# A decoder layer on one core: the first cross-attention stream in another order, the output scaling placed earlier, selection in halves and a final normalisation in pieces

## The reference

```python
x = _layernorm(x + self_attention(x))
# cross attention, 16 heads of 32, causal
q, k, v = (heads(x @ Wq.T + bq), heads(ctx @ Wk.T + bk), heads(ctx @ Wv.T + bv))
Srel = _skew(einsum('bhsd,ld->bhsl', q, Er))
attn = softmax(where(causal, (q @ k.T + Srel) / sqrt(32), -inf))
x = _layernorm(x + (attn @ v))
# routed feed-forward
probs = softmax(einsum('bsd,de->bse', x, Wg) + bg, axis=-2)   # over the 1024 rows
vals, idx = top_k(transpose(probs), 128)
tok = x[bidx, idx]
h = relu(tok @ w1 + b1); h = relu(h @ w2 + b2); h = h @ w3 + b3
out = _layernorm(x + zeros.at[bidx, idx].add(h * vals[..., None]))
```

## Time and profile before

| | us |
|---|---|
| median of 3 runs | 4421.03 |
| lowest, highest | 4416.5, 4429.57 |
| the profiled execution, own time | 4421.36 |
| its span, first to last instruction | 4419.6 |
| busy in it: PE, DVE, ACT, POOL | 3878.7, 2499.9, 1573.0, 908.0 |

### The profile page before, as it was taken

One profiled execution on the slowest core, in us unless ns is written; L12 is line 12 of the kernel. 1 busy time (PEld: TensorE's weight loads), 2 busy tenths in 40 slices (PEclk: granted clock), 3 DMA queues, 4 the chain that ended last, 5 costly groups with the idle time before them and its releaser, 6 DMA issues. The chain is left out here.

```text
span 4419.6 us, 90910 instructions
## 1 busy us (share of the span) xinstructions
PE 3878.7 (88%) x36922; PEld 2372.6 (54%) x36922; DVE 2499.9 (57%) x4789; ACT 1573.0 (36%) x3188; POOL 908.0 (21%) x1023
## 2 busy tenths in 40 slices
PE   6999987899999878999998789999988819999992
PEld 3667544556665346566653566766545504444441
DVE  3777435777773357777723677777246762222224
ACT  2444135744441357444413674444137600000000
POOL 2333101123330011233300112333001102222220
PEclk8999999999999989999999899999998959999996
DMA  8333258634332686333327853433278414454445
GB/s 252 109 90 90 87 222 308 201 104 113 90 85 86 261 293 196 94 109 96 98 76 285 283 168 112 119 95 106 77 281 278 152 60 121 109 132 116 130 114 171
DMA packets 286223, 659.45 MB, mean 149 GB/s; under 512 B 24336, under 2 KB 90816, under 8 KB 282576
## 3 DMA queue, kind: packets, MB, share of 16 engines
q1 hardware_dynamic: 270160, 616.08, 43.2%
q0 software_dynamic: 15344, 35.46, 4.2%
q10 hardware_dynamic: 320, 2.23, 0.1%
HBM read 384.84 MB, written 210.11 MB: 135 GB/s over the span
## 5 line engine op out<-in xcount | busy, mean ns | idle before, releaser
L504 ACT ACTIVATE sc<-sc,nmax 128x1024 f32<-128x1024 f32 x516 | 591.7, 1147 | 797.6 <-DVE nmax L730 797.2
L461 POOL TENSOR_SCALAR sc<-sc,pinv 128x1024 f32<-128x1024 f32 x516 | 577.4, 1120 | 1230.0 <-DVE pinv L738 1217.2
L860 DVE CUSTOM_DVE_ANT_0 sc<-psum,big 128x896 f32<-128x896 f32 (+7 forms) x512 | 362.1, 754 | 217.5 <-PE psum L1221 170.7
L1039 PE MATMUL psum<-pts,wct 32*64 32x256 f32 x8192 | 458.6, 376 | 3.9 <-issue 3.9
L1039 PE MATMUL psum<-xall,wct 32*64 32x256 f32 x8192 | 457.6, 376 | 0.0
L1024 PE MATMUL psum<-xt,w_all 128*128 128x256 f32 x1792 | 415.7, 385 | 23.4 <-PEq L1021 23.4
L504 ACT ACTIVATE sc<-sc,xmax 128x896 f32<-128x896 f32 (+7 forms) x512 | 394.1, 772 | 49.8 <-DVE xmax L860 45.4
L755 DVE STREAM_TRANSPOSE pts<-sc 128x1024 f32<-128x1024 f32 (+3 forms) x342 | 333.6, 975 | 131.4 <-PE psum L1039 87.6
L1024 PEld LDWEIGHTS psum<-xt,w_all 128*128 128x128 f32 x1792 | 332.5, 190 | 128.2 <-issue 66.8
L730 DVE CUSTOM_DVE_ANT_0 sc<-psum,table_a 128x1024 f32<-128x1024 f32 x258 | 312.5, 1211 | 130.1 <-PE psum L986 114.2
L1039 PEld LDWEIGHTS psum<-pts,wct 32*64 32x64 f32 x8192 | 309.5, 132 | 100.8 <-issue 49.9
(11 more groups left out here) (160 smaller groups left out, 5553.0 us busy)
## 6 DMA issues: line engine op xcount, KB each, us to landing
wct<-xall SPq DMA_DIRECT2D x576, 128.0 KB, 2.4
big<-skew_d SPq DMA_DIRECT2D x48, 1024.0 KB, 5.4
w_sb<-w_dram SPq DMA_DIRECT2D x48, 1024.0 KB, 5.4
big<-skew_d SPq DMA_DIRECT2D x48, 768.0 KB, 4.4
big<-skew_d SPq DMA_DIRECT2D x32, 896.0 KB, 4.6
big<-skew_d SPq DMA_DIRECT2D x32, 640.0 KB, 5.2
w_all<-wqkv_dram SPq DMA_DIRECT2D x33, 512.0 KB, 3.6
skew_d<-wct SPq DMA_DIRECT2D x8, 2048.0 KB, 8.1
```

The lines of the kernel that those rows point to most:

```text
L461: pool.tensor_scalar(sc[k % 4][:, :], sc[k % 4][:, :], pinv[:, k % 4:k % 4 + 1], 1.0, ALU.mult, ALU.mult).then_inc(probs_scaled, 1)
L504: act.activation(tile, tile, ACT.Exp, bias=least, scale=-1.0, accum_out=total).then_inc(probs_ready, 1)
L860: dve.tensor_tensor_reduce(scx[u % 2][:, at], SCORES[:, at], skw[u % 4][:, at], -XSCALE, BIG, ALU.add, ALU.min, xmax[:, k:k + 1]).then_inc ...
L1039: mm = pe.matmul(OSUM[HEAD[h], a, :], v_all[rows, ST * (b % GROUPS) + b // GROUPS, HEAD[h]], ptf[h][rows, QG * b:QG * b + QG], start=(b == ...
```

## The change

1. First stream: the row tiles of a quad are made in the order 0, 7, 1, 6, 2, 5, 3, 4 (`REL_ORDER`), and the projections are cut in eighths (`project_eighth`): two ahead of a chunk of 512 columns, one ahead of a smaller one, which is 18 eighths a quad, so that again nine blocks fit in four quads. Buffers rotate by the order made; the places in `skew_d` stay.
2. Second stream: PE turns back right after the scores of the step, ahead of the transposes; DVE scales after the first two additions of the step, ahead of the other additions and of the copies.
3. Selection: the 64 rows are cut in halves of 512 columns on 128 partitions. Each half gives its own sorted 128; the second list is reversed by a matmul with a flipped identity, and the greater of each pair of places is kept. The loads of the logits are four in place of one, and both halves of each row are loaded on both partitions, for the row's maximum and sum.
4. Experts: each sequence's `oute` releases its own scatter, where before one release followed all four.
5. Last normalisation: four buffers, loads in halves as soon as a sequence's last scatter has landed, the scaling on ACT (of the last sequence, odd row tiles on DVE), stores in halves. DVE has two more small operations a sequence (`fbias`).

```diff
-CHUNKS = [(t, n) for t in range(ST) for n in range(0, P * (t + 1), HALF)]
+REL_ORDER = [0, 7, 1, 6, 2, 5, 3, 4]
+CHUNKS = [(t, n) for t in REL_ORDER for n in range(0, P * (t + 1), HALF)]
 NCH = len(CHUNKS)
+FILL = [2 if min(HALF, P * (t + 1) - n) == HALF else 1 for t, n in CHUNKS] * QUADS
+FILLED = [sum(FILL[:kk]) for kk in range(len(FILL) + 1)]
...
-                        if kk % 4 < 3:
-                            p = 3 * (kk // 4) + kk % 4
-                            project_part(3 + p // 4, p % 4)
+                        for i in range(FILLED[kk], FILLED[kk + 1]):
+                            project_eighth(3 + i // ST, i % ST)
                         relative(qd, j)
...
                 for u in range(NU + 4):
                     if u < NU:
                         xscore(u)
+                    for v in range(XV):
+                        if LAST[v] + 3 == u:
+                            turn_back(v)
                     for part in range(2):
...
-                            if part == 0 and LAST[v] + 3 == u:
-                                turn_back(v)
...
+                    for i in range(2):
+                        if u < NU:
+                            add_relative(u, i)
+                    for v in range(XV):
+                        if LAST[v] + 3 == u:
+                            scale_output(v)
                     if u < NU:
-                        for i in range(len(UNITS[u][2])):
+                        for i in range(2, len(UNITS[u][2])):
                             add_relative(u, i)
...
-                                if LAST[v] + 3 == u:
-                                    scale_output(v)
...
-        pr = sf("pr", [ROWS, S])
+        pr = sf("pr", [P, 2, HALF])
+        mine = pr[:, 0, :]
...
+            dve.tensor_copy(lists[:, 0, :], BANK[0][:, 0:P])
+            dve.tensor_copy(lists[:, 1, :], BANK[1][:, 0:P]).then_inc(lists_copied, 1)
+            dve.wait_ge(lists_flipped, 1)
+            dve.tensor_tensor(above[:, :], low_val, high_val, ALU.is_ge)
+            done(dve.tensor_tensor(best_row[:, :], low_row, high_row, ALU.subtract))
+            done(dve.tensor_tensor(best_row[:, :], best_row[:, :], above[:, :], ALU.mult))
+            done(dve.tensor_tensor(best_row[:, :], best_row[:, :], high_row, ALU.add))
...
-                pool.wait_ge(oute_ready, 1)
-                pool.sem_inc(oute_ready, -1)
                 for b in range(B):
+                    pool.wait_ge(oute_ready, b + 1)
...
-            sp.wait_ge(experts_done, 1)
             for b in range(B):
+                sp.wait_ge(scattered[b], 16 * E)
+                for q in range(2):
...
+            def normalize(b):
+                act.wait_ge(fin_scale, b + 1)
+                for t in range(ST):
+                    if not by_dve(b, t):
+                        act.activation(fin[b][:, t, :], fin[b][:, t, :], ACT.Identity, bias=fbias[:, b, t:t + 1],
+                                       scale=finv[:, b, t:t + 1]).then_inc(fin_by_act, 1)
```

More of the change, by code:

```diff
@@ L185, in decoder_layer @@
         bias3 = sbp("bias3", [P, E])
[L186 removed]
+        base_sb = sbp("base_sb", [P, 1])
         stats = sbp("stats", [P, ST, 6])
@@ L259, in block_end @@
         def block_end(kk):
-            return next((r for r in range(3, len(BLOCKS)) if piece_at(4 * (r - 3) + 3) == kk), None)
-        def piece_at(p):
-            return 4 * (p // 3) + p % 3
+            return next((r for r in range(3, len(BLOCKS)) if FILLED[kk] < ST * (r - 2) <= FILLED[kk + 1]), None)
         def probs_t(h, t, first, last):
@@ L1144, in project_part, with project_eighth @@
                         mm.then_inc(block_for_act if ON_ACT[r] else block_for_dve, 1)
+                def project_eighth(r, i):
+                    a, qd = BLOCKS[r]
+                    if i == 0:
+                        pe.wait_ge(*evacuated(r - 2))
+                        if a == 0:
+                            pe.wait_ge(wx_loaded[qd], 16)
+                            pe.sem_inc(wx_loaded[qd], -16)
+                    if a < 2:
+                        n, c = i // DC, i % DC
+                        mm = pe.matmul(psum[:, 2 * (r % 2) + n, :], wxw[qd][:, a, c, :],
+                                       (xt, ct)[a][:, c, HALF * n:HALF * n + HALF], start=(c == 0), stop=(c == DC - 1))
+                    else:
+                        mm = project_xv(r, i)
+                    if i == ST - 1:
+                        mm.then_inc(block_for_act if ON_ACT[r] else block_for_dve, 1)
                 def project_xv(r, t):
@@ L1295, in sf @@
             return ffn.enter_context(nc.sbuf_tensor(name, shape, dt))
-        pr = sf("pr", [ROWS, S])
[L1298 to L1304, removed]
+        pr = sf("pr", [P, 2, HALF])
+        mine = pr[:, 0, :]
+        left = [sf("left0", [P, HALF]), sf("left1", [P, HALF])]
+        top = sf("top", [P, TOPK])
+        top_at = sf("top_at", [P, TOPK], U32)
+        row_no = sf("row_no", [P, TOPK])
+        rmax = sf("rmax", [P, 1])
+        rsum = sf("rsum", [P, 2])
+        rinv = sf("rinv", [P, 1])
+        flip = sf("flip", [P, P])
+        lists = sf("lists", [P, 2, P])
+        above = sf("above", [P, ROWS])
+        best_row = sf("best_row", [P, ROWS])
         vals = sf("vals", [P, B, E])
@@ L1313, in decoder_layer @@
         oute = sf("oute", [P, B, D])
[L1314 to L1319, removed]
+        fin = [sf(f"fin{i}", [P, ST, D]) for i in range(B)]
+        fstats = sf("fstats", [P, B, ST, 6])
+        fmv = sf("fmv", [P, B, ST, 2])
+        fve = sf("fve", [P, B, ST])
+        froot = sf("froot", [P, B, ST])
+        finv = sf("finv", [P, B, ST])
+        fbias = sf("fbias", [P, B, ST])
         BANK = [psum[:, i, :] for i in range(8)]
@@ L1326, in decoder_layer @@
         picks_turned = sem("picks_turned")
+        flip_loaded = sem("flip_loaded")
+        lists_copied = sem("lists_copied")
+        lists_flipped = sem("lists_flipped")
         picks_done = sem("picks_done")
@@ L1423, in _ @@
             act.wait_ge(row_max_ready, 1)
-            act.activation(pr[:, :], pr[:, :], ACT.Exp, bias=rmax[:, :], accum_out=rsum[:, :]
-                           ).then_inc(row_exp_ready, 1)
+            for i in range(2):
+                act.activation(pr[:, i, :], pr[:, i, :], ACT.Exp, bias=rmax[:, :], accum_out=rsum[:, i:i + 1]
+                               ).then_inc(row_exp_ready, 1)
             def copy_tokens():
@@ L1525, in _ @@
             pe.wait_ge(picked, 1)
-            pe.transpose(BANK[0][:, 0:ROWS], row_no[:, :], ident[0:ROWS, 0:ROWS])
-            pe.transpose(BANK[1][:, 0:ROWS], top[:, :], ident[0:ROWS, 0:ROWS]).then_inc(picks_turned, 1)
+            pe.transpose(BANK[0][:, 0:P], row_no[:, :], ident[:, :])
+            pe.transpose(BANK[1][:, 0:P], top[:, :], ident[:, :]).then_inc(picks_turned, 1)
+            pe.wait_ge(flip_loaded, 16)
+            pe.wait_ge(lists_copied, 1)
+            pe.matmul(BANK[2][:, 0:P], flip[:, :], lists[:, :, ROWS:P], start=True, stop=True).then_inc(lists_flipped, 1)
             NT = B * P
@@ L1627 @@
         w3=a["ffn_w3"], b3=a["ffn_b3"],
-        row_base=np.repeat(np.arange(nb) * S, E).astype(np.float32)[:, None], ident_in=np.eye(P, dtype=np.float32))
+        row_base=np.concatenate([np.repeat(np.arange(nb) * S, E) + i * HALF for i in range(2)]
+                                ).astype(np.float32)[:, None],
+        ident_in=np.eye(P, dtype=np.float32), flip_in=np.eye(P, dtype=np.float32)[::-1])
     nc = bacc.Bacc("TRN2", target_bir_lowering=False, num_devices=1)
```

126 lines of the change are left out of this document (72 added, 54 removed).

## The result

The changed kernel takes 4281.08 us (median of 4 runs, 4279.88 to 4284.08) where the kernel before takes 4423.2: a ratio of 0.9677, 95% interval 0.9662 to 0.9693.

What follows compares the result with a forecast made beforehand. Each stretch was given its own bound: PE cycles with copies and store waits, DVE chains, PE in the experts. Terms 50 + 8 + 42 + 8 + 21 + 39.5 = 168.5 us off 4421.4 gave 4253, range 4227 to 4297.

Steps and rivals of the forecast that it cites:

- the second stream: Second stream: next scores and weighing start earlier in the steps from row tile 2 on, 42 us, bounds nothing to 115.
- wrong if PE waits at `turn_back`: Second stream: one of three stated signs that the prediction is wrong, PE waiting at that instruction; no size given.
- First stream: First cross stream: copies hidden better and fewer waits for stores, 50 us, bounds 27 to 55; quad of 30.15 us.
- The fill: First stream: projections in eighths and the new order hide copies better, 1.69 us a quad, 27 us in 16 quads.
- the 23 of stores: First stream: 23 of 28 us put to waits for stores go, as wide and narrow row tiles alternate.
- Border: Border of the streams: last store 1.25 MB instead of 2 MB, SP waits 2.0 us less a sequence, 8 us.
- 42 + 8 us for the order and the clock: Second stream: 42 us from earlier scores and weighing, 8 us from PE's granted clock staying up in later quads.
- a rival for the other sign: Second stream: `turn_back` ahead of the transposes makes PE wait for all exponentials; slower than before, 4445 at 1.5 us each; chance 3.
- Selection and end: Selection: scans of 512 columns instead of 1024, 21 us. End: earlier loads, scaling shared with ACT, 39.5 us.
- my own: Whole kernel: the prediction's own forecast, 4253 us, give or take 20; chance 56 in 100.
- gives little: Second stream: additions or ACT's exponentials replace the wait; a third of the 42, none of the 8; 4289 us; chance 17.
- another rival: Second stream: slower than before, PE waiting at `turn_back` for all exponentials of the last unit; chance 3.

Runs made afterwards that it cites:

- s1_old_fill: The changed kernel with the projections back in quarters behind three of four chunks, new row-tile order kept: 4314.21 us (ratio to before 0.9761).
- s1_both_old: The changed kernel with the first stream as before, row tiles in natural order and projections in quarters: 4348.32 us (ratio to before 0.9836).

## Why the prediction was near, and where it failed

4253 was forecast and 4281 measured, within the range but 28 us from the middle. All of the 28 is one term, the second stream; the others add up to 118.5 forecast and 119.2 measured. By its own sign ("wrong if PE waits at `turn_back`") that term's account failed, and the range held because it was wide enough, not because it allowed for this.

**First stream: right.** 51.6 for 50. The fill measured 24.7 in the new order for 27; before's stream less that of s1_old_fill gives 26.9 for the 23 of stores. (Against s1_both_old it is 33.7, so the stores' part is known to some 7 us only.) The quad is 30.3 for 30.2. Only the two don't add up from either side: in the natural order the eighths bring 14.3 of their 24.7.

**Border: right in sum, for half the reason.** SP at the border, in the timeline of the changed kernel:

```profile
690.09 0.36 SPq L400 DMA_DIRECT2D skew_d<-wct  x1
694.67 2.50 SPq L412 DMA_DIRECT2D wct<-xall  x4
```

It waits 4.6 us for the last store where it was 6.6, the 2.0 that I took. The second unit's step gained 3.7 a sequence, and the gap ahead of the first addition lost 1.3: with the eighths the last projection block is copied behind the last chunk. Net 9.5 over four sequences for 8. In s1_old_fill, which ends on the same 1.25 MB, SP waits 5.9 us (697.15 to 703.07), and 6 of the 9.5 are gone. So the size of the last store brought 0.7 of the 2.0 us, and the rest came with the eighths; why the last store lands sooner with them was not tried apart.

**Second stream: the step that failed.** I took 42 + 8 us for the order and the clock, and charged PE's new wait for `copy_ot` at 0.3 in one step of a quad, 4.8 us in all. The gain was as computed: row tile 2 lost 0.96 (0.96 forecast), row tile 3 1.09 (1.2), and without the price of `turn_back` the four steps from row tile 2 on lose 18.57 less 15.38 = 3.19 a quad, the 3.2 of the sum. The price was mis-sized: the matmuls waited 34.7 us, and with what hangs on them it came to 36. It is 0.53 in row tiles 0 and 1, 1.31 in the first step of row tile 4 (5.18 against 3.87), and 1.6 more in 6 of 16 quads where the clock fell behind it: 12 later quads at 1.84 are 22, the six falls 10, and the first quads bring the 36 to which the two streams differ (753.1 less 717.1). I had the wait as a rival for the other sign, with the earlier trace rows against it, and priced it as all or nothing. Rows 9 were read wrongly: the little wait at the old place told of a copy that half of the transposes hid, in steps 1 us longer. Neither holds once the step is shortened and the instruction moved ahead of its cover.

Priced by whole kernels, the order as changed gave 12 us, and with `turn_back` left alone it gives 54 (4292.9 to 4238.6), the whole term of 42 + 8. How it divides between the order and the clock was not tried apart.

**Selection and end: right.** 47 scans at 0.53 less are 25; the rest of the difference to 20.2 is the load (8.18 us for 6.66 from issue to reduction) and the three us of merging at its end. The end gave 39.9 for 39.5. ACT's tile measured 0.72 where 0.6 was assumed, hidden in both cases. Release by sequence (10.8) and scaling on ACT (9.2) are shown one by one; what of the remaining 20 is the four buffers and what the halves was not tried apart.

**The chances.** The case that came true lies between my own and the first rival, "gives little": 22 of the 50 came by the traces, for a reason that stands in the text under another rival.

## What to carry to other kernels

When a step is shortened, look again at every wait that it used to hide: here ACT's copy was on time only while the step before took 1 us longer. Move an instruction ahead of its cover only if its input is ready there in the new timing, not in the old; in an in-order queue what counts is what stands in front of the producer. Where several engines share the work of a step, try the moves one by one: here one of the two held the whole gain, and the other only cost.

For transfers, the order in which big and small buffers are stored can matter as much as their sum: the same bytes a quad made the copies wait up to 5.6 us and PE 3.4 in natural order; in alternation one wait of 1.5 is left in the whole kernel.

## What was not expected of the hardware

In one stretch of the changed first stream the DMA engines moved more than I took as full use (353 GB/s from the earlier trace rows):

```profile
582.00:590.00 8.00, 7.39 (x40) 2.61 (x40) 3.14 (x3) 3.27 (x4) 0.00 (x0) 1.00 0.92 352
590.00:598.00 8.00, 7.62 (x54) 3.91 (x46) 3.55 (x4) 2.61 (x3) 0.00 (x0) 1.00 0.98 374
```

This 374 GB/s is also above the 358 of the Trainium skill, "DMA: Bandwidth & Descriptors", section "Where 436 GB/s comes from". That section makes the figure by halving a stack's 716 between two cores, and this program runs on one.

In the changed kernel PE stood for 1.21 to 1.23 us at `turn_back` in 13 of the 16 first steps of row tile 4. Behind 6 of these stops the granted clock fell from 2.4 to 1.2 GHz, behind 7 it stayed up; behind the three shorter ones (0.74 to 1.03) it stayed up too. What decides between them stays open.
